# Four banks for the value products, another hand-over and a written-out tail in a fused GRU, attention, Runge-Kutta and FFN kernel

## What is computed

```python
# GRU, 64 steps, state (32, 512)
gi = x @ W_ih + b_ih;  gh = h @ W_hh + b_hh          # (32, 1536) each
r = sigmoid(i_r + h_r); z = sigmoid(i_z + h_z)
n = tanh(i_n + r * h_n);  h = (1 - z) * n + z * h
# attention: layernorm * gamma, rotary, 16 query heads of 128, one key/value head
x = x + (softmax(causal(q k^T * 128**-0.5)) v) @ Wo
# Runge-Kutta: 64 steps of four derivatives, q and p (32, 512), drive = x of the step
dq = q - q**3 / 3 - p + drive + tanh(q) @ coupling.T + bias
dp = 0.08 * (q + 0.7 - 0.8 * p)
q, p = clip(rk4(q, p), -20, 20)                       # q of each step goes on
# FFN on the 2048 rows of q, inner width 1408, rows quantised to fp8 (e4m3) by their maximum
t = silu(qlinear(q, w_gate)) * qlinear(q, w_up)
x = x + qlinear(quantised(t), w_down)
```

## Time and profile before

| | us |
|---|---|
| median of three runs | 1581.16 |
| fastest and slowest run | 1580.62, 1585.36 |
| the profiled execution | 1583.37 |
| its span (first to last instruction) | 1581.6 |
| PE busy | 1493.9 (94%) |
| PEld busy | 933.0 (59%) |
| DVE busy | 1067.5 (67%) |
| ACT busy | 589.1 (37%) |
| POOL busy | 474.6 (30%) |

### The profile page before, as it was taken

One profiled execution on the slowest core, in us unless ns is written; L12 is line 12 of the kernel. 1 busy time (PEld: TensorE's weight loads), 2 busy tenths in 40 slices (PEclk: granted clock), 3 DMA queues, 4 the chain that ended last, 5 costly groups with the idle time before them and its releaser, 6 DMA issues.

```text
span 1581.6 us, 45959 instructions
## 1 busy us (share of the span) xinstructions
PE 1493.9 (94%) x16649; PEld 933.0 (59%) x16690; DVE 1067.5 (67%) x3437; ACT 589.1 (37%) x1917; POOL 474.6 (30%) x673
## 2 busy tenths in 40 slices
PE   5999999998899999999999999999999999999985
PEld 1333333334775758576767664766666666666662
DVE  1666766775764545464555552578999999899986
ACT  2444444553021020202020112455565566555552
POOL 0212121111220202020211110245566555656650
PEclk9999999998999999999999999999999999999997
DMA  8121122214300000000000105011111111111111
GB/s 309 45 51 48 45 53 60 65 39 148 42 1 7 20 12 14 27 0 27 0 27 0 27 5 213 26 29 40 34 37 34 49 45 33 37 33 37 35 46 39
DMA packets 91139, 72.68 MB, mean 46 GB/s; under 512 B 32824, under 2 KB 83000, under 8 KB 89912
## 3 DMA queue, kind: packets, MB, share of 16 engines
q1 hardware_dynamic: 71256, 59.09, 12.6%
q10 hardware_dynamic: 18048, 6.89, 1.7%
q0 software_dynamic: 1760, 5.77, 1.3%
HBM read 54.76 MB, written 16.94 MB: 45 GB/s over the span
## 4 chain that ended last, share of the span: by engine, by line
PE 71%; DVE 19%; issue 4%; ACT 4%; DMA 1%; SPq 0%; DVEq 0%; POOLq 0%; POOL 0%; ACTq 0%
PE ps L767 14%; PE ps L665 11%; PE ps L677 11%; PE ps L737 10%; PE ps L875 9%; DVE mem L1429 3%; PE ps L806 3%; DVE mem L1480 3%; PE ps L830 3%; ACT mem L1117 2%; DVE ps L1456 2%; PE ps L891 1%; DVE mem L1604 1%; DVE mem L1470 1%; DVE mem L1612 1%
## 5 line engine op out<-in xcount | busy, mean ns | idle before, releaser
L875 PE MATMUL ps<-mem 128*32 128x128 f32 x8192 | 277.9, 276 | 28.0 <-ACT mem L1117 18.5
L875 PEld LDWEIGHTS ps<-mem 128*32 128x32 f32 x8192 | 210.5, 110 | 102.3 <-ACT mem L1117 70.1
L582 POOL TENSOR_TENSOR mem<-mem 128x256 f32<-128x256 f32 x128 | 92.9, 726 | 450.3 <-DVE mem L1338 450.3
L767 PE MATMUL ps<-mem 128*128 128x256 f32 x1024 | 222.3, 379 | 0.0
L767 PEld LDWEIGHTS ps<-mem 128*128 128x128 f32 x1024 | 193.9, 190 | 26.0
L665 PE MATMUL ps<-mem 128*32 128x384 f32 x2048 | 181.8, 497 | 9.6 <-DMA mem<-in_W_ih 5.8
L677 PE MATMUL ps<-mem 128*32 128x384 f32 x2048 | 177.6, 487 | 2.4 <-DVE mem L1258 2.4
L737 PE MATMUL ps<-mem 128*128 128x512 f32 x384 | 168.7, 592 | 0.0
L1075 ACT ACTIVATE mem<-mem 128x512 f32<-128x512 f32 x32 | 19.7, 630 | 386.8 <-DVE mem L1370 386.8
L1117 ACT ACTIVATE mem<-mem 128x64 f32<-128x64 f32 x512 | 110.3, 250 | 90.6 <-DVE mem L1429 84.8
L865 PE MATMUL ps<-mem 128*128 128x128 f32 x768 | 137.5, 302 | 1.6
(11 more groups left out here) (152 smaller groups left out, 2172.1 us busy)
## 6 DMA issues: line engine op xcount, KB each, us to landing
mem<-x_scr SPq DMA_DIRECT2D x127, 64.0 KB, 1.8
mem<-in_xT SPq DMA_DIRECT2D x64, 64.0 KB, 1.9
mem<-in_Wq SPq DMA_DIRECT2D x1, 4096.0 KB, 12.5
mem<-in_Wo SPq DMA_DIRECT2D x1, 4096.0 KB, 15.3
q_scr<-mem SPq DMA_DIRECT2D x64, 64.0 KB, 1.6
mem<-q_scr SPq DMA_DIRECT2D x64, 64.0 KB, 1.9
out<-mem SPq DMA_DIRECT2D x64, 64.0 KB, 1.6
mem<-in_W_ih SPq DMA_DIRECT2D x1, 3072.0 KB, 10.0
```

Of the source, the lines that this page charges most:

```text
L582: pool.tensor_tensor(one, one, turned[h % 2].rearrange("p (b t) -> p b t", t=T), ALU.add).then_inc(qr_done, 1)
L767: mm = pe.matmul(ps[:, h % Q_BANKS, 0:BLK], wq[:, c, h * DH:(h + 1) * DH], xnb[:, c, :], start=(c == 0), stop=(c == NC - 1))
L875: mm = pe.matmul(ps[32 * j:32 * j + 32, st % 2, 0:P], thT[:, c, :], ct[:, c, j * P:(j + 1) * P], start=False, stop=(c == NC - 1), skip_gro ...
```

## The change

1. **Start.** SP issues `W_ih` without waiting for the biases; `W_hh` comes in four transfers, each with a semaphore of its own, and `h_part` of the first step waits for each quarter. TensorE gets two more products whose result nobody reads, behind the two that spread the biases.
2. **Value products.** `PV_BANKS` has a fourth bank, bank 4. Product n waits for the copy of product n - 4 instead of n - 3, and only from the fifth on. DVE builds `bias_ps` after the last of these copies.
3. **Hand-over.** SP issues `own_drive`, the rows of the scratch array and the drives ahead of the FFN weights. The drive sum for the second step moves from the first stage to the fourth. One output piece of the last block fewer is made before the stages and two slots give up a piece; one slot kind takes five pieces instead of four; the second late residual moves one slot on. ACT runs a one-column Silu after its last copy of attention. ACT's groups stand in a loop of one turn.
4. **Slots.** The first quarter of product 5 moves from slot 0 to slot 1.
5. **Tail.** The three last tiles get a `tail` of their own on each engine instead of the groups with `rk` false. POOL adds the output of tile 13, and adds and rounds the first half of tile 14; the down products of tile 15 go to bank 2 and start when its first half is there; the output of tile 14 is scaled and added after the last rounding of tile 15.

The diff, cut to its core (the first `tail` in it is POOL's, the second TensorE's, the last lines are DVE's; ACT has one in the same manner; y, a and z are tiles 13, 14 and 15):

```diff
-PV_BANKS = (5, 2, 3)
+PV_BANKS = (5, 2, 3, 4)
...
-            0: ((4, 0, NC), (5, 0, 1)), 1: ((5, 1, NC),), 3: ((6, 0, NC),), 4: ((7, 0, NC),)}
+            0: ((4, 0, NC),), 1: ((5, 0, NC),), 3: ((6, 0, NC),), 4: ((7, 0, NC),)}
...
+LAST_BANK = 2
...
-EARLY_HEADS = {6: 8, 7: 5}
-LATE_SLOTS = (3, 2, 1, 4)
-LATE_FREE = [(0, k) for k in range(16)] + [(1, k) for k in range(11)] + [(2, k) for k in (2, 5, 6, 7, 8, 9, 10)]
+EARLY_HEADS = {6: 8, 7: 4}
+LATE_SLOTS = (3, 2, 1, 5)
+LATE_FREE = [(0, k) for k in range(16)] + [(1, k) for k in (0, 1, 2, 3, 4, 5, 6, 7, 8, 10)] + [(2, k) for k in (2, 5, 6, 7, 8, 9)]
...
-            sp.wait_ge(b_ld, 32)
             sp.dma_start(wih, W_ih.rearrange("p (c n) -> p c n", c=NC)).then_inc(wih_ld, 16)
-            for half, ld in enumerate(whh_ld):
-                rows = slice(2 * half, 2 * half + 2)
-                sp.dma_start(whh[:, rows, :], W_hh.rearrange("p (c n) -> p c n", c=NC)[:, rows, :]).then_inc(ld, 16)
+            for c, ld in enumerate(whh_ld):
+                sp.dma_start(whh[:, c, :], W_hh.rearrange("p (c n) -> p c n", c=NC)[:, c, :]).then_inc(ld, 16)
...
             for j in range(NC):
                 sp.dma_start(drive[0][32 * j:32 * j + B - BLK_B, :], x1_scr[0, j, 0:B - BLK_B, :]).then_inc(drive_ld[0], 16)
-            sp.wait_ge(ws_wr, 16)
-            sp.dma_start(wgT, wgu_scr[0]).then_inc(ffn_ld, 16)
-            sp.wait_ge(s_mm, 2 * PAIRS * NBLK)
-            half_x_rows(NBLK - 1, 1, late_x)
-            sp.dma_start(wuT, wgu_scr[1]).then_inc(ffn_ld, 16)
-            sp.dma_start(wdT, wd_scr).then_inc(ffn_ld, 16)
...
+            sp.wait_ge(s_mm, 2 * PAIRS * NBLK)
+            half_x_rows(NBLK - 1, 1, late_x)
+            sp.wait_ge(ws_wr, 16)
+            sp.dma_start(wgT, wgu_scr[0]).then_inc(ffn_ld, 16)
+            sp.dma_start(wuT, wgu_scr[1]).then_inc(ffn_ld, 16)
+            sp.dma_start(wdT, wd_scr).then_inc(ffn_ld, 16)
+            for row, lo, hi in ((gs_row, 0, IC), (us_row, IC, 2 * IC), (ds_row, 2 * IC, 2 * IC + NC)):
+                sp.dma_start(row, scale_scr[lo:hi, :].rearrange("k p -> (k p)").partition_broadcast(P)).then_inc(ffn_ld, 16)
...
+            def tail():
+
+                y, a, z = LAST
+                gate_scaled(a, 2)
+                gate_scaled(a, 3)
+                output(y)
+                for m in range(GU_T):
+                    gate_scaled(z, m)
+                lo, hi = T_PARTS[0]
+                pool.wait_ge(f_te, 1)
+                pool.tensor_tensor(vt[:, lo:hi], vt[:, lo:hi], et[:, lo:hi], ALU.add).then_inc(f_ta, 1)
+                t_rounded(a, 0)
+            tail()
 
...
+            for _ in range(2):
+
+                pe.matmul(ps[:, 2, :], xt[0].rearrange("p c b -> p (c b)"), bias_bc, start=True, stop=True)
...
-                    if c % 2 == 0 and first:
-                        pe.wait_ge(whh_ld[c // 2], 16)
+                    if first:
+                        pe.wait_ge(whh_ld[c], 16)
...
-                            if n >= 3:
-
-                                pe.wait_ge(ao_cp, 4 * PAIRS * blk + n - 2)
-                            pe.matmul(ps[:, PV_BANKS[n % 3], :], vtok[64 * b2:64 * b2 + 64, pr, :], pT[64 * b2:64 * b2 + 64, half * 512:(half + 1) * 512],
+                            if n >= 4:
+
+                                pe.wait_ge(ao_cp, 4 * PAIRS * blk + n - 3)
...
+            act.activation(sig[1][:, 0:1], identf[:, 0:1], ACT.Silu)
...
+            dve.wait_ge(ao_cp, 4 * PAIRS * NBLK)
...
                     fill()
-                elif not end:
+                if not end and st == (0 if t else 3):
...
+            def tail():
+
+                y, a, z = LAST
+                product(a, 4, 0, NC)
+                product(a, 5, 0, NC)
+                t_turned(y, 1)
+                product(a, 6, 0, NC)
+                product(a, 7, 0, NC)
+                downs(y, 7)
+                x_turned(z)
+                pe.wait_ge(f_qTcp, z + 1)
+                for order in range(2 * GU_T):
+                    product(z, order, 0, NC)
+                t_turned(a, 0)
+                t_turned(a, 1)
+                downs(a, 7)
+                t_turned(z, 0)
+                pe.wait_ge(f_gated, GU_T * z + GU_T)
+                pe.wait_ge(f_tTcp, 2 * z + 1)
+                down(0, T_PARTS[0][1] // P, LAST_BANK)
+                t_turned(z, 1)
+                pe.wait_ge(f_tTcp, 2 * z + 2)
+                down(T_PARTS[0][1] // P, IC, LAST_BANK)
...
+                v = Steps(dve, rk_v, counts["next"])
+                gate_part(a, 2)
+                gated_part(a, 1)
+                gate_part(a, 3)
+                part_max(v, a, 0)
+                part_max(v, a, 1)
+                gated_part(a, 2)
+                part_max(v, a, 2)
+                x_scale(v, z)
+                gated_part(a, 3)
+                x_grid(v, z)
+                dve.wait_ge(f_xe, z + 1)
+                dve.tensor_tensor(vq, vq, eq, ALU.add).then_inc(f_xa, 1)
+                dve.wait_ge(f_xa, z + 1)
+                dve.wait_ge(f_qT, z)
+                dve.tensor_tensor(qx8, vq, eq, ALU.subtract).then_inc(f_q8, 1)
+                part_max(v, a, 3)
+                t_scale(v, a)
+                dve.wait_ge(f_gated, GU_T * a + GU_T)
+                v.did(dve.tensor_copy(xsx, xnew))
+                y_scaled(v, y, 7)
+                dve.wait_ge(f_ysc, y + 1)
+                v.need(v.did(dve.tensor_copy(tsy, tsx)))
+                gate_part(z, 0)
+                gate_part(z, 1)
+                t_bits(v, a, 0)
+                t_grid(v, 0, f_te)
+                gated_part(z, 0)
+                gate_part(z, 2)
+                dve.wait_ge(f_vt, 2 * a + 2)
+                gated_part(z, 1)
+                gate_part(z, 3)
+                part_max(v, z, 0)
+                gated_part(z, 2)
+                part_max(v, z, 1)
+                t_bits(v, a, 1)
+                t_grid(v, 1)
+                gated_part(z, 3)
+                part_max(v, z, 2)
+                part_max(v, z, 3)
+                t_scale(v, z)
+                dve.wait_ge(f_ta, 2 * a + 1)
+                t_added(v, 1)
+                dve.wait_ge(f_t8, 2 * a + 1)
+                t_rounded(a, 1)
+                for half in range(2):
+                    t_bits(v, z, half)
+                    t_grid(v, half)
+                    t_added(v, half)
+                    t_rounded(z, half)
+                y_scaled(v, a, 7)
+                dve.wait_ge(f_ysc, a + 1)
+                dve.wait_ge(x1_ld, 16 * TILE_T * (a + 1))
+                dve.wait_ge(o_wr, PRIMED + 16 * TILE_T * a)
+                dve.tensor_tensor(yout, ysc, x1t, ALU.add).then_inc(f_out, 1)
+                v.did(dve.tensor_copy(tsy, tsx))
+                y_scaled(v, z, LAST_BANK)
+                dve.wait_ge(f_ysc, z + 1)
+                dve.wait_ge(x1_last, 16 * TILE_T)
+                dve.tensor_tensor(ysc, ysc, qt, ALU.add).then_inc(f_out, 1)
```

213 lines of the change are left out of this document (121 added, 92 removed).

## The result

The changed kernel takes 1557.38 us (median of four runs, 1556.88 to 1561.95) against 1582.39 us before (four runs, 1580.62 to 1585.36): a ratio of 0.9847 with a 95% interval of 0.9821 to 0.9872. The forecast of 1547 us with a range of 1541 to 1556 was too low: the gain is 25.0 us between the medians (24.2 by the ratio), 34.9 were summed. The profiled execution has a span of 1555.9 us, 25.7 less than before, so the two traces account for all of it.

What follows compares the result with a forecast made beforehand. TensorE was taken to hold most of the chain of waits, with VectorE setting the pace after 1536 us. Terms 4.6 + 15.0 + 7.9 + 0.4 + 7.0 = 34.9 off the 1581.16 median gave 1546.3, rounded to 1547; range 1541 to 1556.

Steps and rivals of the forecast that it cites:

- The start, 4.6: GRU start: earlier W_ih, full-rate x products and W_hh in quarters end the h products at about 20.9, not 25.5 us.
- W_ih 1.9 us earlier, and its landing with it: Start: W_ih, issued at 2.6 us without the wait for the biases, lands at 12.7 instead of 14.5.
- Value products, 15.0: Attention: with a fourth bank, products 2 and 3 run as a pair, saving 0.94 us in each of 16 groups.
- Rival (a): Value products: the bank removes the wait but product 3 still runs by itself; 6.7 us instead of 15.0, 1555; chance 0.15.
- Hand-over, 7.9: Attention to Runge-Kutta: 6.9 us from earlier small transfers, drive sum and clock, 0.5 from table load, 0.5 from moved pieces.
- loop, 0.4: Runge-Kutta slots: one quarter product moved from slot 0 to slot 1 gains 0.4 us over the kernel, bounds -2 and +3.
- rival (d): Slower than before: FFN weights behind the drives hold up first-group stores, drive loads and their own readers; 1585 us, chance 0.02.
- In by 995: Hand-over: FFN weights, asked for at about 975, land by 995; first reader at about 1007, a cover of 12 us.
- The end, 7.0: Tail: VectorE work moved to GpSimd or behind the last rounding gains 7.5, less 0.5 for GpSimd contention; bounds 4 and 10.
- I laid the new order out with the durations of the old rows: Tail: by old durations, the last rounding ends 26.9 us after 1536.1 instead of 33.9, 7.0 us earlier.
- (b): Clock not won: x products, first stages and end stay at low rate; 6.5 us lost, 1553; chance 0.13.
- (c): Everything at full rate at the end and W_hh never late: 3.5 us better, 1543; chance 0.08.

## Why the prediction was wrong

The mechanisms were right and none of the rivals came true as it was written, but the sum was too large by 9.2 us: 3.3 at the start, 1.7 at the value products, 2.4 at the hand-over and in the loop, 1.8 at the end. In its order:

**The start, 4.6: wrong in size, and the largest miss.** 3.4 us were there at the first ScalarE work, 1.3 at the first value product. The first step that failed is "W_ih 1.9 us earlier, and its landing with it": it landed 1.2 us earlier, and W_hh at 21.2 and not at 20.2. The weights now share the transfer engines with the biases (the DMA share from 4 to 8 us is 1.09, before 0.79, and 1.03 in both from 8 to 12); that this is what made them late was not tested. Of the 3.4 us 1.3 went back by the third step, whose hole of 3.9 us I had passed over because it was in both kernels: the clock is low behind it, or already at the step before, and with the new start that costs 1.3 to 1.6 us more in each execution as long as the hole stays. Another 0.8 went to the low clock ahead of the first value product. With that hole and the wait behind Wq gone, the GRU ends 5 us earlier. And the two products, which I gave most of the term, are worth 0.6 us: the last quarter of W_hh covers the rest. I had them at 3.75 us and running up to W_ih; they took 2.31 and TensorE was idle for 2.41 us behind them, and the clock held all the same.

**Value products, 15.0: the step held, 13.3 in the changed kernel and 13.6 by the kernel with the bank alone.** Thirteen groups give the 0.94 or a little over, 12.4 together. From the first to the second, at the low clock, 0.36 is won, and in the last block TensorE meets ScalarE's half copies, which the 0.6 us of cover did not count: 0.64 and 0.58 of new waiting leave 0.3 for each of its two groups. Rival (a) is out. The caution that the copies out of PSUM may come to bound row-tiled products (the Trainium skill, "TensorEngine Tiling (Array Packing)", Performance Considerations) bears on that last block alone, by the 0.64 and 0.58 us behind ScalarE; in the thirteen groups the copies stay hidden.

**Hand-over, 7.9, and loop, 0.4: 5.9 together.** The first stage came 2.5 us earlier in itself instead of 3.7, since I counted one issue of 0.4 us where ScalarE's two take 1.94. The drive sum, the clock and the table load came as worked out: the first two stages take 2.2 us each instead of 4.1 and 3.8, and stage 29, which had the table load, 2.2 instead of 2.7. Stage 9's stall took 1.2 us back, and it is what rival (d) should have been: the weights behind the drives did hurt, not their own readers or SyncE's queue but TensorE in the middle of its products. "In by 995" was right (they were in by about 980), and it was not the cover that counted.

**The end, 7.0: 5.2.** The step that failed is "I laid the new order out with the durations of the old rows". The last rounding comes 3.6 us sooner, not 7.0. 2.4 of the 3.4 us between them are VectorE's own masking and scaling, stretched next to GpSimd. I took 0.5 off for GpSimd's side of the contention and nothing for VectorE's. The rest goes with the clock at tile 15's gate and up products, for which I had no term: they begin 11.2 us after the last stage in all eight profiled executions with this tail, but the last rounding ends 30.6 to 30.8 us after it in the three in which the first eight of them ran at full rate, 32.1 to 32.2 in the four in which they ran at half rate, and 31.6 in one between. From the last stage to the end the eight lie between 40.2 and 42.1 us, so in four of them the end gains 6.8 to 7.1 us, as forecast, and in this one 5.2. Behind the rounding it is the other way round: 6.5 us to the last add instead of 8.1, a gain of 1.6 where I had 0.5. The Trainium skill, "SBUF — State Buffer", section "SBUF: two separate sides", has an exclusive lock for operations that need the shared ports: whichever of the two engines starts first gets it for its whole instruction, and the other waits. I had used that for GpSimd only; the trace agrees with it for VectorE too, whose scaling starts at 1534.60 inside a GpSimd operation (1534.11 to 1535.95), ends 0.4 us behind it and takes 1.77 us instead of 0.56.

**The range.** It held rivals (a), (b) and (c) one at a time, but four terms read from best cases fell short at once; of such a case only (a) with (b) was named, and left outside. Run to run the kernel moves by up to 5 us besides (1556.9 to 1562.0).

## What to carry to other kernels

Price a contended resource from both sides: work that is moved to a second engine also slows the first where they run side by side. Bulk loads beside a tight serial loop may be worth issuing one at a time with gaps, even when their data is wanted much later: here it gave 3.3 us. Time won ahead of a hole that stays need not be kept in full: close the hole first, and look for what its wait is really for. Where idle time comes just ahead of work on TensorE, give the clock a term of its own.
